# The recurrent part's first output product: VectorE's and ScalarE's opening order written out by hand

## What is computed

```
x = layernorm(x, ln0_w, ln0_b)                      # the input norm
for l in range(4):
    h = layernorm(x, ln1_w[l], ln1_b[l]);  hh = time_shift(h)
    k, v, sr = (h and hh mixed by tmk / tmv / tmr) @ Wk[l], Wv[l], Wr[l];  sr = sigmoid(sr)
    x = x + (sr * wkv(time_decay[l], time_first[l], k, v)) @ Wo[l]      # the output product
    h = layernorm(x, ln2_w[l], ln2_b[l]);  hh = time_shift(h)
    kf = square(relu((h and hh mixed by cmk) @ Wck[l]))
    x = x + sigmoid((h and hh mixed by cmr) @ Wcr[l]) * (kf @ Wcv[l])
```

## Time and profile before

| | |
|---|---|
| median of three runs | 1873.02 us |
| the profiled execution | 1874.18 us |
| its span, first to last instruction | 1872.4 us |
| busy: PE / DVE / ACT | 1753.7 / 1250.4 / 958.5 us |
| mean granted TensorE clock | 0.970 |

### The profile page before, as it was taken

One profiled execution on the slowest core, in us unless ns is written; L12 is line 12 of the kernel. 1 busy time (PEld: TensorE's weight loads), 2 busy tenths in 40 slices (PEclk: granted clock), 3 DMA queues, 4 the chain that ended last, 5 costly groups with the idle time before them and its releaser, 6 DMA issues.

```text
span 1872.4 us, 27207 instructions
## 1 busy us (share of the span) xinstructions
PE 1753.7 (94%) x10508; PEld 1535.1 (82%) x10508; DVE 1250.4 (67%) x1923; ACT 958.5 (51%) x1479; POOL 3.6 (0%) x26
## 2 busy tenths in 40 slices
PE   2499999999999998898899999999999999999997
PEld 1277887877888787887798989989899889998896
DVE  6989999999999865888544454544544445444445
ACT  3588898888889773343333333333333333233323
POOL 0000000000000000000000000000000000000000
PEclk9699999999999998999699999999999999999999
DMA  3010010001000002110200111000100010010001
GB/s 118 0 46 18 12 41 22 7 7 57 6 12 29 0 29 88 43 54 11 88 21 14 35 35 34 32 2 34 34 34 34 0 34 34 34 56 16 1 1 40
DMA packets 34702, 56.59 MB, mean 30 GB/s; under 512 B 3030, under 2 KB 20412, under 8 KB 33596
## 3 DMA queue, kind: packets, MB, share of 16 engines
q1 hardware_dynamic: 34620, 55.47, 9.1%
HBM read 51.79 MB, written 3.67 MB: 30 GB/s over the span
## 4 chain that ended last, share of the span: by engine, by line
PE 50%; DVE 1%; ACT 0%; issue 0%; ACTq 0%; DVEq 0%
PE fbanks L1691 17%; PE fbank L1691 16%; PE fbank L1707 16%; ACT acc L1662 0%; DVE acc L1546 0%; PE fbank L52 0%; DVE fst L1572 0%; DVE xk L1570 0%; PE fbanks L1724 0%; ACT acc L1639 0%; DVE fmv L1575 0%; ACTq L1369 0%; DVE hl L1529 0%; DVE fyy L1586 0%; DVE frstd L1587 0%
## 5 line engine op out<-in xcount | busy, mean ns | idle before, releaser
L1522 DVE TENSOR_TENSOR hf<-sil,fbanks 128x512 f32<-128x512 f32 (+1 forms) x128 | 79.4, 620 | 332.9 <-PE fbanks L1691 274.2
L1630 ACT ACTIVATE sil<-fbanks 128x512 f32<-128x512 f32 (+1 forms) x128 | 69.6, 544 | 442.2 <-PE fbanks L1691 442.2
L1707 PE MATMUL fbank<-wl,hh 128*128 128x256 f32 x896 | 250.3, 279 | 0.0
L1707 PE MATMUL fbank<-wh,hl 128*128 128x256 f32 x896 | 250.1, 279 | 0.0
L1707 PE MATMUL fbank<-wh,hh 128*128 128x256 f32 x896 | 250.1, 279 | 0.0
L1522 DVE TENSOR_TENSOR hf<-sil,fbank 128x512 f32<-128x512 f32 (+1 forms) x128 | 79.5, 621 | 150.3 <-PE fbank L1691 143.3
L1707 PEld LDWEIGHTS fbank<-wl,hh 128*128 128x128 f32 x896 | 168.3, 188 | 2.2
L1707 PEld LDWEIGHTS fbank<-wh,hh 128*128 128x128 f32 x896 | 168.4, 188 | 1.8
L1707 PEld LDWEIGHTS fbank<-wh,hl 128*128 128x128 f32 x896 | 168.4, 188 | 0.0
L728 PE MATMUL pair<-wcvh,kfh 128*112 128x256 f32 x512 | 149.6, 292 | 12.2 <-DVE kfl L404 12.1
L1630 ACT ACTIVATE sil<-fbank 128x512 f32<-128x512 f32 (+1 forms) x128 | 69.7, 545 | 177.2 <-PE fbank L1691 177.2
(11 more groups left out here) (235 smaller groups left out, 3801.7 us busy)
## 6 DMA issues: line engine op xcount, KB each, us to landing
raw<-in_w_gate SPq DMA_DIRECT2D x16, 512.0 KB, 3.9
raw<-in_w_up SPq DMA_DIRECT2D x16, 512.0 KB, 4.7
raw<-in_w_down SPq DMA_DIRECT2D x16, 512.0 KB, 5.7
raw<-in_w_ck SPq DMA_DIRECT2D x4, 1024.0 KB, 4.9
raw<-in_w_cv SPq DMA_DIRECT2D x4, 1024.0 KB, 4.9
raw<-in_ctx_t SPq DMA_DIRECT2D x4, 750.0 KB, 6.0
ct<-in_ctx_t SPq DMA_DIRECT2D x4, 750.0 KB, 5.0
x<-in_x SPq DMA_DIRECT2D x4, 448.0 KB, 6.4
```

The lines of the kernel that those rows point to most:

```text
L1522: dve.tensor_tensor(hf[i][:, 0:w], sil[i][:, 0:w], bank[2 * i + 1][:, 0:w], ALU.mult).then_inc(hf_ready, 1)
L1630: act.activation(sil[f % 2][:, 0:w], bank[2 * (f % 2)][:, 0:w], ACT.Silu).then_inc(sil_ready, 1)
L1707: ins = pe.matmul(bank[4 + 2 * (t % 2) + i // 2][:, (i % 2) * C:(i % 2 + 1) * C], a[t % 2][:, f, i * P:(i + 1) * P], m[h][:, DOWN + f * C: ...
```

## The change

Turns s = -3 to -1 of VectorE's and ScalarE's loops are taken out and written as straight lists ahead of a loop that begins at s = 0. TensorE's program is the same. What the lists do otherwise:

- The scaling of the input norm of groups 1, 2 and 3 goes from VectorE (`normalise`, four operations) to ScalarE (`normalise(0, m)`, four, in place), with a `set_shift(0)` on VectorE and two semaphore counters (`shift_ready[0]`, `xn_ready[0]`). Group 0 stays as it was. The multiplication by `ln0_w` and the addition of `ln0_b` stay on VectorE.
- `stats` of groups 2 and 3 stand one place earlier, `input_norm(3)` stands behind `wkv_arguments(1)`, and `wkv_out(0)` stands ahead of `input_norm(2)`.
- The first `high_weights(0, "ck")` and `low_weights(0, "ck")` stand in the opening list instead of turn s = 0.
- On ScalarE the tanh of step 0 and its two table loads stand behind the exponentials of step 0, and ahead of its reciprocal.
- SyncE issues the first `w_ck` behind x of group 1, x of group 2 behind it, and x of group 3 behind wr.

```diff
@@ sync
+            load_x(0)
             (ln0w, ln0b, prm)
+            load_x(1)
             for l in range(STEPS // GROUPS):
+                load_stage(l, "ck")
                 if l:
-                    load_stage(l, "ck")
                     load_stage(l, "cv")
+                else:
+                    load_x(2)
                 for n, tile, used, per in uses:
...
                     if l == 0 and n == "r":
-                        load_stage(l, "ck")
+                        load_x(3)
@@ vector
+            def input_stats(m):
+                dve.wait_ge(x_in[m], 16)
+                if m >= 2:
+                    dve.wait_ge(shift_ready[0], m - 1)
+                stats(0, chunk(m))
+            def input_norm(m):
+                dve.wait_ge(xn_ready[0], m)
+                scale_and_bias(m)
...
-            first_norm(0)
-            for s in range(-3, STEPS + 1):
+            input_stats(0); rsqrt(0, 0); after(normalise(0, chunk(0))); scale_and_bias(0)
+            stats(1, chunk(0)); input_stats(1); rsqrt(1, 0); set_shift(1)
+            rsqrt(0, 1); set_shift(0); input_stats(2)
+            low_weights(0, "ck", wckl, wckh, ck_done, 4)
+            mix1(0); input_norm(1); stats(1, chunk(1))
+            rsqrt(0, 2); set_shift(0); input_stats(3)
+            wkv_arguments(0); rsqrt(1, 1); set_shift(1)
+            wkv_sums(0); wkv_denominator(0); wkv_numerator(0)
+            mix1(1); wkv_gated(0); wkv_out(0)
+            input_norm(2); stats(1, chunk(2)); rsqrt(0, 3); set_shift(0)
+            wkv_arguments(1); rsqrt(1, 2); set_shift(1)
+            input_norm(3); wkv_sums(1)
+            for s in range(STEPS + 1):
...
-                    if s % GROUPS == 0:
+                    if s and s % GROUPS == 0:
                         low_weights(s // GROUPS, "ck", wckl, wckh, ck_done, 4)
...
-                if s + 4 < GROUPS:
-                    first_norm(s + 4)
@@ scalar: normalise(k, m) writes x itself where k is 0, and waits for shift_ready[0] >= m
             rsqrt0(0, 0)
-            for s in range(-3, STEPS + 1):
+            high_weights(0, "ck", wckh, ck_done, 4)
+            rsqrt0(1, 0); rsqrt0(0, 1); normalise(1, 0); norm_out(1, 0, ...)
+            normalise(0, 1); rsqrt0(0, 2); out(0, 0, kp, ...); rsqrt0(1, 1); out(0, 1, v, ...)
+            wkv_exp(0, 0); wkv_exp(0, 1); wkv_exp(0, 2); normalise(1, 1); norm_out(1, 1, ...)
+            preload(EXP_TANH); out(0, 2, th, ..., ACT.Tanh, 0.5); preload(LN_EXP)
+            reciprocal0(0); normalise(0, 2); rsqrt0(0, 3); out(1, 0, kp, ...)
+            act.wait_ge(num_ready, 1); out(1, 1, v, ...)
+            preload(EXP_TANH); out(1, 2, th, ..., ACT.Tanh, 0.5); preload(LN_EXP)
+            rsqrt0(1, 2); normalise(0, 3)
+            wkv_exp(1, 0); wkv_exp(1, 1); wkv_exp(1, 2); normalise(1, 2)
+            for s in range(STEPS + 1):
...
-                    if s % GROUPS == 0:
+                    if s and s % GROUPS == 0:
                         high_weights(s // GROUPS, "ck", wckh, ck_done, 4)
```

More of the change, by code:

```diff
@@ L114, in rwkv_phase @@
         rstd = {k: sb(f"rstd{k}", [T, G]) for k in (0, 1, 2)}
-        shift = {k: sb(f"shift{k}", [T, G]) for k in (1, 2)}
+        shift = {k: sb(f"shift{k}", [T, G]) for k in (0, 1, 2)}
         xn, h, mixed = {}, {}, {}
@@ L200, in sync, with load_x @@
             xv = io["x"].rearrange("b t c -> t b c")
-            for c in range(GROUPS):
+            def load_x(c):
                 sp.dma_start(x[:, c * G:(c + 1) * G, :], xv[:, c * G:(c + 1) * G, :]).then_inc(x_in[c], 16)
[L203 to L206, removed]
+            load_x(0)
+            sp.dma_start(ln0w[:], io["ln0_w"].partition_broadcast(T)).then_inc(params_in, 16)
+            sp.dma_start(ln0b[:], io["ln0_b"].partition_broadcast(T)).then_inc(params_in, 16)
+            sp.dma_start(prm[:, :, :, 0:NPRM_IN], io["prm"]).then_inc(params_in, 16)
+            load_x(1)
             uses = (("k", wk, kvr_done, 3), ("v", wv, kvr_done, 3), ("r", wr, kvr_done, 3), ("o", wo, wo_done, 1),
@@ L447, in vector @@
             dve.wait_ge(w_ready, 5)
-            first_norm(0)
-            for s in range(-3, STEPS + 1):
+            input_stats(0)
+            rsqrt(0, 0)
+            after(normalise(0, chunk(0)))
+            dve.wait_ge(params_in, 48)
+            scale_and_bias(0)
+            stats(1, chunk(0))
+            input_stats(1)
+            rsqrt(1, 0)
+            set_shift(1)
+            rsqrt(0, 1)
+            set_shift(0)
+            input_stats(2)
+            low_weights(0, "ck", wckl, wckh, ck_done, 4)
+            mix1(0)
+            input_norm(1)
+            stats(1, chunk(1))
+            rsqrt(0, 2)
+            set_shift(0)
+            input_stats(3)
+            wkv_arguments(0)
+            rsqrt(1, 1)
+            set_shift(1)
+            wkv_sums(0)
+            wkv_denominator(0)
+            wkv_numerator(0)
+            mix1(1)
+            wkv_gated(0)
+            wkv_out(0)
+            input_norm(2)
+            stats(1, chunk(2))
+            rsqrt(0, 3)
+            set_shift(0)
+            wkv_arguments(1)
+            rsqrt(1, 2)
+            set_shift(1)
+            input_norm(3)
+            wkv_sums(1)
+            for s in range(STEPS + 1):
                 if valid(s):
@@ L539, in normalise @@
             def normalise(k, m):
-                act.wait_ge(shift_ready[k], m + 1)
+                act.wait_ge(shift_ready[k], m + 1 if k else m)
                 xc = x[:, (m % GROUPS) * G:(m % GROUPS + 1) * G, :]
+                dst = xn[k] if k else xc
                 for i in range(G):
-                    ins = act.activation(xn[k][:, i, :], xc[:, i, :], ACT.Identity, bias=shift[k][:, i:i + 1],
+                    ins = act.activation(dst[:, i, :], xc[:, i, :], ACT.Identity, bias=shift[k][:, i:i + 1],
                                          scale=rstd[k][:, i:i + 1])
@@ L615, in scalar @@
             rsqrt0(0, 0)
-            for s in range(-3, STEPS + 1):
+            high_weights(0, "ck", wckh, ck_done, 4)
+            rsqrt0(1, 0)
+            rsqrt0(0, 1)
+            normalise(1, 0)
+            norm_out(1, 0, pair[2], "ln1w", "ln1b")
+            normalise(0, 1)
+            rsqrt0(0, 2)
+            out(0, 0, kp[:, :, :, 1:T1], k_out)
+            rsqrt0(1, 1)
+            out(0, 1, v[:], v_out)
+            wkv_exp(0, 0)
+            wkv_exp(0, 1)
+            wkv_exp(0, 2)
+            normalise(1, 1)
+            norm_out(1, 1, pair[2], "ln1w", "ln1b")
+            act.preload_act_table_set(EXP_TANH)
+            out(0, 2, th[:], th_ready, ACT.Tanh, 0.5)
+            act.preload_act_table_set(LN_EXP)
+            reciprocal0(0)
+            normalise(0, 2)
+            rsqrt0(0, 3)
+            out(1, 0, kp[:, :, :, 1:T1], k_out)
+            act.wait_ge(num_ready, 1)
+            out(1, 1, v[:], v_out)
+            act.preload_act_table_set(EXP_TANH)
+            out(1, 2, th[:], th_ready, ACT.Tanh, 0.5)
+            act.preload_act_table_set(LN_EXP)
+            rsqrt0(1, 2)
+            normalise(0, 3)
+            wkv_exp(1, 0)
+            wkv_exp(1, 1)
+            wkv_exp(1, 2)
+            normalise(1, 2)
+            for s in range(STEPS + 1):
                 if valid(s):
@@ L655, in scalar @@
                     act.preload_act_table_set(LN_EXP)
-                if s >= 0 and valid(s + 3):
+                if valid(s + 3):
                     rsqrt0(1, s + 3)
```

15 lines of the change are left out of this document (3 added, 12 removed).

## The result

The changed kernel took 1858.64 us (median of four runs, 1858.57 to 1858.96), against 1873.37 us in four runs of the kernel before: ratio 0.9923, interval 0.9905 to 0.994. Run again beside 25 runs of the kernel before it gave 1858.17 against 1871.55 us, ratio 0.9923 (0.9906 to 0.994).

What follows compares the result with a forecast made beforehand. VectorE's list was taken to bound the opening, until TensorE is busy throughout from 137.89 us. Blocks A to E (7.7 us) plus F (3.1) gave 10.8 us, so 1862.5 us; own range 1861 to 1864.5, 8-in-10 range 1859.5 to 1867.

Steps and rivals of the forecast that it cites:

- blocks A to E: Opening, from the statistics at 15.57 us to the first sum onto x: VectorE's list 7.7 us earlier.
- the cover of 0.55 us: VectorE's slack left before the first dk at 23.53 us, after the weight split is fitted into its former wait.
- The scaling's share: Opening: scaling of groups 1 to 3 leaves VectorE, 3 x 1.42 us, with shifts of 3 x 0.2 coming back.
- the product's nine microseconds: Output product starting at 63.3 instead of 73.05 us: worth nothing in itself, done six before VectorE comes for it.
- the shorter wait for the first h: Before the first mix1: VectorE's 4.78 us wait shrinks to 0.55 as dk starts at 23.53 instead of 28.72.
- the three start values: Opening: VectorE's three waits for ScalarE's start value of a norm, about 0.65 us each, go.
- block F: Turn s = 0: without the weight split, 0.9 us less waiting before ckl and 2.2 us of VectorE's work, 3.1 us.
- it is carried to the sixteenth round: Behind 137.89 us TensorE is nearly always busy, so the opening's 10.8 us gain is carried to the end.
- the rest of the span unchanged: After the projections starting at 127.1 instead of 137.89 us, the remaining span keeps its length.
- more than forecast: Rival: TensorE without its slow stretch starts the steps better, 1859 to 1861 us, chance 0.07.
- Rival 3: Slower: TensorE's granted clock falls in attention or at the experts' start through a phase shift, 1877 us, chance 0.04.

## Why the prediction was wrong

**Right: blocks A to E.** 7.7 us worked out, 7.83 measured, each block within 0.15 us, the cover of 0.55 us found as a wait of 0.47. The scaling's share is shown by undoing it (3.09 against 3.2). That the product's nine microseconds count for nothing by themselves is read from the trace, as VectorE reached the sum with no wait in either kernel. What is left of the 7.8 us, the shorter wait for the first h and the three start values that aren't waited for any more, was not undone by itself; it is read from the two timelines.

**Right: block F,** 3.1 us. The split alone gives 3.16, undoing it takes 3.1 in the two lines meant. In the profile pair it was 3.42, as TensorE's first projection of step 2 took 4.04 us instead of 4.38 behind its idle stretch. That is luck of the pair: the same projection took 3.91 to 5.41 us in the fourteen profiles, the longer the lower its granted clock (0.79 at 4.04, 0.73 at 4.38, 0.61 at 5.21, 0.59 at 5.41), the last two of these in the change with the old layout and in the second profile of the kernel before. VectorE's wait for mix_ck follows: 2.11, 2.44, 3.28 and 3.48 us. I had no term for this; it is worth a microsecond either way in a single profile.

**Right: it is carried to the sixteenth round.** In the old layout the change gives 10.06 us there against the first profile of the kernel before, with a wait for mix_ck that was 0.84 us longer (3.28 against 2.44), and 11.03 against the second, whose wait (3.48) is nearly the same; 10.8 stood. The medians of that kernel differ by 9.9. My reasoning that the first 137.89 us are the opening holds; only the round that begins there is the fourth and not the third.

**Wrong: "the rest of the span unchanged".** This step failed. From the first profile, 10.8 us less would have given a span of 1861.6 us; it was 1856.8. Of the 4.8 us between them, 0.2 are the earlier start and 0.5 the luck in block F and the small excess of blocks A to E. The other 4.1 lie in the rest of the span, in two parts.

The first is the channel product's pace, 1.3 us over the recurrent part, from the tile that the change adds: I read the diff's `shift = {... (0, 1, 2)}` as bookkeeping and gave it neither a term nor a bound. The tile alone and the change without it show this. My rival "more than forecast" had the right sign, another mechanism, and a chance of 0.07.

The second part, 2.9 us, lies behind the sixteenth round of projections, where the time goes with TensorE's granted clock. There the first profile of the kernel before is of the longest kind, 1257.4 us; the changed kernel took 1254.5, the second profile of the kernel before 1252.9. I had one profile, and took what lies behind the opening as a fixed number. Rival 3 named clock and attention as the place where the time can shift with no instruction changed, but only towards slower. That this part is due to the change isn't shown: it is smaller than what two runs of one kernel differ by. Against the second profile, the changed kernel's is 11.8 us shorter in all: 12.3 in the opening (1.4 by the projections' clock), 1.2 by the layout, 1.6 lost behind the sixteenth round, and 0.1 by a later start.

The medians hold the same in other shares. The runs of the kernel before sit near 1870.5 or 1873.6, and two of the three beside the first profile, and so their median, were of the upper heap. From the lower heap the changed kernel (1858.2) is 12.3 us away, from the upper one 15.4. That 12.3 is near the forecast's 10.8 plus the layout's 1.3 isn't proof of either, as the stretches behind them differ. The range's lower end, 3 us below the forecast, had room for the first part and not for both.

Not settled: what in the ck tiles' place sets the pace; what decides between the three lengths, and whether the change has a part in it.

## What to carry to other kernels

Walk the list of the engine that holds up the start: between operations common to both kernels the walk was good to 0.15 us, and an early output that its reader comes for late is worth nothing. But a new tile, even of 16 bytes, moves every tile behind it. Where a product runs hundreds of times back to back, test the layout by itself, with the tile alone and no instruction changed, before an order of instructions gets the credit. And look at several runs of the kernel before for heaps, take a second profile if there are any, and compare the stretches that the change doesn't touch, before a sum is set against one profile or one median.

## What the runs showed of the hardware

- Forty-eight fp32r matmuls of 448 columns took 9.90, 10.00 or 10.09 us in most steps, by the place of tiles alone (the moving operand 0 or 64, 96, 32 bytes beyond a multiple of 128), with 9.80 in two steps of the slowest layout. They start 199 to 207 ns apart, in rounds that differ from place to place. The experts' part didn't change for moves of 32 or 64 bytes (951.5 us in all).
- The same projection behind eight to eleven idle microseconds of TensorE and a turn took 3.91 us at a mean granted clock of 0.81, 4.38 at 0.73 and 5.41 at 0.59; the last two are of one kernel.
- What lies behind the sixteenth round of projections took 1257.4 us in one profile of a kernel and 1252.9 in another of the same kernel, with granted clocks of 0.97 and 0.98, 0.92 and 0.93, 0.90 and 0.92 in the stretches that differ.
- A load of 1 MB issued third among the large ones was in at 11.2 us.
